# A two-layer decoder on one core: the last rows of the gated product are normalised inside the quantised stage

## The reference, cut to what matters

```
x = layernorm(x + attention(x))                  # 16 heads
x = layernorm(x + cross_attention(x, context))   # 16 heads, causal
x = layernorm(x + gated_mlp(x))                  # silu(x Wg) * (x Wu) Wd, width 1024
x = layernorm(x + quantised_attention(x))        # int4 activations in chunks of 32 rows, 32 heads
x = layernorm(x + grouped_attention(x, context))
x = layernorm(x + eight_bit_product(x))
```

## Time and profile before

| | |
|---|---|
| median of 3 runs | 2766.9 us (2765.09, 2766.90, 2777.92) |
| profiled execution | 2765.41 us, of which the span of the profile is 2763.6 us |
| busy in the span | PE 95%, DVE 69%, ACT 51%, POOL 43% |
| granted TensorE clock, mean | 0.972 |

### The profile page before, as it was taken

The page is one execution under the profiler, slowest core; times in us unless marked ns, Lnnn a source line. Parts: engine busy times, 40 slices in busy tenths (PEclk is TensorE's granted clock), DMA queues, the critical chain, the costliest instruction groups (busy, mean ns, idle before and its releaser), DMA issues. The chain is left out here.

```text
span 2763.6 us, 66143 instructions
## 1 busy us (share of the span) xinstructions
PE 2625.6 (95%) x23860; PEld 2277.5 (82%) x23860; DVE 1911.1 (69%) x4152; ACT 1413.9 (51%) x3352; POOL 1183.4 (43%) x1559
## 2 busy tenths in 40 slices
PE   7999999997899999999999969999699999999996
PEld 7999999995798888888988858888477777777775
DVE  6655565564777777777777745444599899867775
ACT  3222222223666666666666643332466666666664
POOL 2211111113667767767677630111234444444443
PEclk9999999998999999999999989999799999999997
DMA  5000000001000000000000020000100000001100
GB/s 192 9 8 8 4 8 8 8 0 62 5 6 4 4 6 4 4 6 4 6 4 4 4 80 1 0 0 0 39 9 13 8 11 11 20 29 43 38 30 24
DMA packets 43394, 49.65 MB, mean 18 GB/s; under 512 B 3952, under 2 KB 33616, under 8 KB 43056
## 3 DMA queue, kind: packets, MB, share of 16 engines
q1 hardware_dynamic: 43312, 48.55, 5.3%
HBM read 35.96 MB, written 4.19 MB: 15 GB/s over the span
## 5 line engine op out<-in xcount | busy, mean ns | idle before, releaser
L588 POOL TENSOR_TENSOR a_probs<-a_probs,a_rs 128x512 f32<-128x512 f32 x64 | 70.6, 1103 | 466.4 <-DVE a_rs L444 466.4
L1174 POOL TENSOR_TENSOR b_rows<-b_rows,b_swapped 128x512 f32<-128x512 f32 x160 | 204.7, 1288 | 56.5 <-DVE b_swapped L947 56.5
L1109 ACT ACTIVATE b_probs<-bank,b_shift,b_q_scale 128x128 f32<-128x128 f32 x512 | 228.2, 461 | 0.7
L532 ACT COPY a_pT<-bank 128x512 f32<-128x512 f32 x64 | 37.5, 586 | 308.4 <-PE bank L325 308.4
L1221 POOL TENSOR_TENSOR b_probs<-b_probs,b_rs 128x512 f32<-128x512 f32 x128 | 133.2, 1041 | 137.3 <-DVE b_rs L999 134.1
L449 DVE TENSOR_TENSOR a_oT<-bank,a_oT 128x512 fp32r<-128x512 f32 x128 | 82.5, 686 | 143.6 <-ACT a_oT L537 143.6
L955 DVE TENSOR_REDUCE b_ss<-b_squares 128x4 f32<-128x512 f32 x192 | 125.2, 680 | 73.7 <-ACT b_squares L1084 73.7
L1184 POOL TENSOR_TENSOR b_rms<-b_rms,sh_minus_half 128x8 f32<-128x8 f32 (+1 forms) x128 | 170.4, 1331 | 10.6
L46 PE MATMUL bank<-a_xT,early_wq 128*128 128x256 f32 x512 | 150.2, 293 | 13.2 <-DVE early_wq L73 10.4
L46 PE MATMUL bank<-early_wo,b_oT 128*128 128x256 f32 x512 | 150.7, 294 | 1.4 <-DVE b_oT L921 1.4
L46 PE MATMUL bank<-early_wo,a_oT 128*128 128x256 f32 x512 | 145.3, 284 | 4.0 <-DVE a_oT L449 4.0
(11 more groups left out here) (386 smaller groups left out, 9049.0 us busy)
## 6 DMA issues: line engine op xcount, KB each, us to landing
d_x_in<-sh_x SPq DMA_DIRECT2D x32, 256.0 KB, 2.4
a_xT_in<-in_xT SPq DMA_DIRECT2D x16, 256.0 KB, 2.7
sh_x<-in_x SPq DMA_DIRECT2D x1, 4096.0 KB, 18.1
b_ctx_in<-in_ctxT SPq DMA_DIRECT2D x32, 128.0 KB, 2.0
e_cT<-in_ctxT SPq DMA_DIRECT2D x32, 128.0 KB, 2.5
out<-f_res SPq DMA_DIRECT2D x16, 256.0 KB, 2.6
a_qT<-in_L_attn_Wq SPq DMA_DIRECT2D x4, 512.0 KB, 6.2
a_stage<-in_L_attn_Wo SPq DMA_DIRECT2D x1, 2048.0 KB, 13.0
```

The lines of the kernel that those rows point to most:

```text
L1109: op = act.activation(probs[:, g % 2, keys], bS[:, keys], ACT.Exp, bias=shift[:, g % 2, a:a + 1], scale=q_scale[:, g, a // 2, a % 2:a % 2 ...
L1174: pool.tensor_tensor(rows[:, unit, :], rows[:, unit, :], swapped[:, half, :], ALU.add).then_inc(added[unit], 1)
```

## The change

1. The gated block ends with the last residual sum. The moments of its last four tiles are taken by DVE as its first work of the next block (`late_stats`), and POOL normalises them during the first turn of the quantised stage, after `find_spans` of that turn (`late_normalise`). `WideRows` is made before both blocks.
2. In the first turn PE turns the two tiles from `sh.x` instead of `x_in`. The load of the first two tiles is still issued. SP waits, ahead of the load for the second turn, until the late normalisation is done.
3. The product with the value bias comes behind the first turning of rows; DVE adds it in the first turn, after `centre`. PE's three waits move from ahead of the turns to a place in the first turn, ahead of `spread_top`.
4. POOL clears `g_v` in its second turn, after `find_spans`.
5. The rows of the last sublayer's result (`f_res`) use the memory of the quantised weights' rows.

```diff
+def late_stats(dve, rows, n_tiles, done):
+
+    for r in range(n_tiles):
+        dve.bn_stats(rows.stats[:, r, :], rows.res[:, r, :]).then_inc(done, 1)
+    dve.wait_ge(done, n_tiles)
+    for r in range(n_tiles):
+        dve.bn_aggr(rows.meanvar[:, r, :], rows.stats[:, r, :]).then_inc(done, 1)
+
+
+def late_normalise(pool, rows, first_tile, n_tiles, stats_done, step, before):
+
+    n = n_tiles
+    pool.wait_ge(stats_done, 2 * n)
+    pool.tensor_scalar(rows.rstd[:, 0:n], rows.meanvar[:, 0:n, 1], LN_EPS, None, ALU.add).then_inc(step, 1)
+    pool.wait_ge(step, before + 1)
+    pool.tensor_tensor(rows.rstd[:, 0:n], rows.rstd[:, 0:n], rows.minus_half[:, 0:n], ALU.pow).then_inc(step, 1)
...
+    pool.tensor_tensor(rows.res[:, 0:n, :], rows.res[:, 0:n, :],
+                       rows.rstd[:, 0:n].unsqueeze(2).to_broadcast([128, n, D]), ALU.mult).then_inc(step, 1)
+    pool.wait_ge(step, before + 4)
+    pool.tensor_tensor(rows.x[:, first_tile:first_tile + n, :], rows.res[:, 0:n, :],
+                       rows.shift[:, 0:n].unsqueeze(2).to_broadcast([128, n, D]), ALU.subtract).then_inc(step, 1)
+    pool.wait_ge(step, before + 5)
...
@@ gated_mlp_block @@
-        wide = WideRows(sh, sb, NR)
+        wide = sh.wide
...
             turn(n_turns - 1, None, n_turns - 2)
-            row_stats(dve, wide, n_turns - 1, NR, res_ready, stats_ready, meanvar_ready)
...
-            with pool.Fori(0, n_turns) as i:
+            with pool.Fori(0, n_turns - 1) as i:
                 normalise(pool, wide, i, NR, meanvar_ready, norm_step, norm_done)
@@ tail_block @@
-        f_res = f_sb("res", [128, 2, 2, D])
+        f_res = sh.quantised.rows[:, 0:2]
...
             sh.eight.load(sp, t)
+            sp.wait_ge(zeroed, 12)
+            sp.wait_ge(x_loaded, nth(0, 1, 1, 16))
             with sp.Fori(1, n_turns) as i:
...
             pe.wait_ge(w_loaded, 16 * sh.quantised.N_LOADS)
-            for c in range(C):
-                op = pe.matmul(bP[:, 0:D], v_bias[:, c:c + 1].to_broadcast([128, 128]), w[:, O, c, :], start=(c == 0), stop=(c == C - 1))
-            op.then_inc(v_bias_through, 1)
+            def is_first(i):
+                return i is not None and type(i.n) is int and i.n == 0
+
+            def carry_v_bias():
+                for c in range(C):
+                    op = pe.matmul(bP[:, 0:D], v_bias[:, c:c + 1].to_broadcast([128, 128]), w[:, O, c, :], start=(c == 0), stop=(c == C - 1))
+                op.then_inc(v_bias_through, 1)
...
-                pe.wait_ge(x_loaded, nth(i.n, 1, 1, 16))
+                rows = sh.x if is_first(i) else x_in
+                if not is_first(i):
+                    pe.wait_ge(x_loaded, nth(i.n, 1, 1, 16))
...
-                        op = pe.transpose(bX[0][:, c * 256 + r * 128:c * 256 + (r + 1) * 128], x_in[:, r, c * 128:(c + 1) * 128], sh.ident[:, :])
+                        op = pe.transpose(bX[0][:, c * 256 + r * 128:c * 256 + (r + 1) * 128], rows[:, r, c * 128:(c + 1) * 128], sh.ident[:, :])
                 op.then_inc(qx.turned, 1)
+                if is_first(i):
+                    carry_v_bias()
...
                 turn_cmax_x(new)
+                if is_first(new):
+                    pe.wait_ge(out_bias_ready, 9)
+                    pe.wait_ge(of_chunk_ready, 1)
+                    pe.wait_ge(zeroed, 7)
                 turn_cmax_att(old)
                 spread_top(new, qx, bX[1], y_summed)
...
         def _(dve):
+            late_stats(dve, sh.wide, sh.wide.N, out_bias_ready)
             dve.wait_ge(w_loaded, 16 * sh.quantised.N_LOADS)
-            dve.wait_ge(v_bias_through, 1)
-            dve.tensor_tensor(out_bias[:, :], bP[:, 0:D], b_out[:, :], ALU.add).then_inc(out_bias_ready, 1)
+            def carry_bias():
+                dve.wait_ge(v_bias_through, 1)
+                dve.tensor_tensor(out_bias[:, :], bP[:, 0:D], b_out[:, :], ALU.add).then_inc(out_bias_ready, 1)
...
                 centre(new, qx, bX[0])
+                if new is not None and type(new.n) is int and new.n == 0:
+                    carry_bias()
...
             pool.wait_ge(zeroed, 7)
-            pool.memset(g_v[:, :, :, :, :], 0.0).then_inc(zeroed, 1)
-            pool.wait_ge(zeroed, 8)
-            for h in range(2):
-                pool.memset(g_v[h * S:(h + 1) * S, :, :, :, 2 * W + h:2 * W + h + 1], 1.0).then_inc(zeroed, 1)
             pool.wait_ge(w_loaded, 16 * sh.quantised.N_LOADS)
-            pool.wait_ge(zeroed, 10)
...
                 find_spans(new, qx)
+                if is_turn(new, 0):
+                    late_normalise(pool, sh.wide, NT - sh.wide.N, sh.wide.N, out_bias_ready, zeroed, 7)
+                if is_turn(new, 1):
+                    clear_values()
                 weigh_steps(new, qx)
```

More of the change, by code:

```diff
@@ L147, in normalise @@
     pool.sem_inc(norm_done, 1)
+def late_stats(dve, rows, n_tiles, done):
[10 more added lines that the diff above has]
+    pool.tensor_tensor(rows.rstd[:, 0:n], rows.rstd[:, 0:n], rows.minus_half[:, 0:n], ALU.pow).then_inc(step, 1)
+    pool.wait_ge(step, before + 2)
+    pool.tensor_tensor(rows.shift[:, 0:n], rows.meanvar[:, 0:n, 0], rows.rstd[:, 0:n], ALU.mult).then_inc(step, 1)
+    pool.tensor_tensor(rows.res[:, 0:n, :], rows.res[:, 0:n, :],
[4 more added lines that the diff above has]
+    pool.wait_ge(step, before + 5)
 def self_attention_block(nc, sh):
@@ L1248, with __init__, sb @@
 class WideRows:
-    def __init__(self, sh, sb, n):
+    N = 4
+    def __init__(self, sh, nc, ctx):
+        def sb(name, shape):
+            return ctx.enter_context(nc.sbuf_tensor("wide_" + name, shape, F32))
+        n = self.N
         self.x, self.minus_half, self.passed_dve, self.passed_pool = sh.x, sh.minus_half, sh.passed_dve, sh.passed_pool
@@ L1952, in _ @@
             pe.wait_ge(w_ready, 4)
-            pe.wait_ge(out_bias_ready, 1)
-            pe.wait_ge(of_chunk_ready, 1)
-            pe.wait_ge(zeroed, 7)
             def g_turn_x(i, oldest):
@@ L2244, in _ @@
             pe.wait_ge(g_w_loaded, 16 * sh.grouped.N_LOADS)
-            pe.wait_ge(zeroed, 10)
+            pe.wait_ge(zeroed, 15)
             from_first_to_second()
@@ L3009, in _, with is_turn, clear_values @@
             pool.wait_ge(zeroed, 7)
-            pool.memset(g_v[:, :, :, :, :], 0.0).then_inc(zeroed, 1)
-            pool.wait_ge(zeroed, 8)
-            for h in range(2):
-                pool.memset(g_v[h * S:(h + 1) * S, :, :, :, 2 * W + h:2 * W + h + 1], 1.0).then_inc(zeroed, 1)
             pool.wait_ge(w_loaded, 16 * sh.quantised.N_LOADS)
-            pool.wait_ge(zeroed, 10)
+            def is_turn(i, n):
+                return i is not None and type(i.n) is int and i.n == n
+            def clear_values():
+                pool.memset(g_v[:, :, :, :, :], 0.0).then_inc(zeroed, 1)
+                pool.wait_ge(zeroed, 13)
+                for h in range(2):
+                    pool.memset(g_v[h * S:(h + 1) * S, :, :, :, 2 * W + h:2 * W + h + 1], 1.0).then_inc(zeroed, 1)
+                pool.wait_ge(zeroed, 15)
             def find_bias(i, q):
@@ L3458, in program @@
             sh.quantised, sh.grouped, sh.eight = QuantisedWeights(nc, late), GroupedWeights(nc, late), EightBitWeights(nc, late)
+            sh.wide = WideRows(sh, nc, late)
             for sublayer in REST:
```

## The result

The changed kernel took 2755.7 us, median of 7 runs (2750.66 to 2761.33), against 2767.5 us for the kernel before in the same comparison (7 runs, 2764.88 to 2779.04). The ratio is 0.9945, 95% interval 0.9923 to 0.9966. A second measurement of the same kernel gave 2757.2 us (6 runs) against 2771.8 (26 runs), ratio 0.9957, 0.9941 to 0.9973. In microseconds the ratios are 15.2 (9.4 to 21.3) and 11.9 (7.5 to 16.4). They are not the quotients of the two medians, which lie 11.8 and 14.6 us apart. The forecast was 12.9 of gain and 2753.0 us.

The account below looks back on a forecast made before the run. The prediction held PE to bound the quantised stage (408 of 435 us), with a one-engine-at-a-time chain at the seam. 12.3 us there plus 0.6 for the clock made 12.9, hence 2753.0 us, range 2748 to 2760.

Parts of the forecast that it names:

- earlier start of the block: At the seam, the gated block ends with the residual sum, so the next block starts 7.46 us earlier.
- waits within the start: Between block start and POOL's bias work, shorter waits of POOL, PE and DVE give 4.9 us.
- The crossing: Between the two blocks: last operation to first of the next assumed to cost 1.07 us also when DVE is last.
- The marker: POOL's start on the bias in the first turn, L3022: forecast at 1939.2 instead of 1951.5, 12.3 us earlier.
- Taking only the load away would not have given it: At the block's start, removing the load alone would not gain the 4.9 us, since `of_chunk` ended PE's wait.
- Late normalisation hidden by 0.7 us: On POOL between `find_spans` and `weigh_steps`: 5.83 us fit into 6.53 of idleness, cost 0, bounds 0 to 1.9.
- the sign named in the prediction: On POOL in the first turn: `weigh_steps` starting straight behind the normalisation would show the prediction wrong.
- Clock, 0.6 us: PE's clock in the first turns: gain from less idleness ahead, 0.6 us taken for all.
- Rival A: First turn: DVE's `unit` or inversion waits for POOL's last normalising operation, up to 1.9 us, time 2755; 15%.
- Rival C: Block start: another engine or ACT's and SP's semaphores hold it; gain 8.0 us, time 2758; 6%.
- Rival D: Later turns: slow clock granted in most, 2.73 us each, slower from the fifth more, 2780 with ten; 2%.
- Rival B: Later turns: one or two slow-clock turns more or fewer, 2.73 us each, time 2747.5 to 2758.5; 27%, evenly.

Follow-up runs that it names:

- after: Profiled execution of the changed kernel in the first measurement, the slowest of its seven runs: 2761.33 us.
- `of_chunk` ahead: Changed kernel, but PE waits for ACT's `of_chunk` ahead of its first turn, rows still turned from `sh.x`; 2765.9 us, one run.
- the short filling: Changed kernel plus 6, 8 and 7 unread PE products behind the value bias, top's spread and first scores of the first turn; 2756.2 us, ratio 0.9943.
- again: Profiled execution of the unchanged changed kernel in its second measurement, the fastest of its runs: 2751.74 us.
- the extra power: Changed kernel plus one more power of 4 columns (1.04 us) on POOL ahead of the late normalisation; 2761.6 us, one run.
- an earlier start: Changed kernel with POOL's clearing of `v` moved into the first turn and DVE's lowest and highest ahead of the late moments; 2749.3 us, ratio 0.9938.
- the filled kernel: Changed kernel plus 26 unread PE products in the first turn, 12 behind the value bias, 14 behind `spread_top`; 2759.8 us, ratio 0.9954.
- the load put back: Changed kernel, but in the first turn PE waits for the load into `x_in` and turns the tiles from there; 2758.0 us, one run.

## Why the prediction was right, by its steps

The mechanism was the one forecast, and the parts can be set beside the terms ("after"; places are relative to the end of the residual sum):

| step of the prediction | forecast | measured |
|---|---|---|
| earlier start of the block | 7.46 us, with a crossing of 1.07 | 8.53 - 0.82 = 7.71, crossing 0.82 |
| waits within the start | 4.9 | 8.32 - 3.47 = 4.85 |
| spans to `weigh_steps`, with the late normalisation in it | 0 (6.53 hides 5.83) | 6.16 instead of 6.53, 0.37 gained; 0.08 us to spare |
| first projection to value projection | part of the clock's 0.6 | 5.18 to 4.75, 0.43 gained |
| sum | 12.9 | 13.4; 12.9 of it to the first projection, where 12.3 were forecast |

The level, 2753.0 us, was missed by 2.7 and 4.2 us (2755.7 and 2757.2). Part of that is the starting point: the forecast took 2766.9 us of three runs for the kernel before, and the later medians were 2767.5 and 2771.8. Whether the gain is within 0.5%, to which the prediction gave 0.60, is not settled: the two ratios stand at 0.55% and 0.43%.

- *The crossing.* The one assumption made for want of a row. It was 0.81 to 0.82 us in every kernel whose block ended with DVE's sum, and 1.07 again in the one that ended with POOL.
- *The marker.* 1938.43, forecast 1939.2. Of the difference 0.53 us are that execution's earlier residual sum and 0.25 the crossing.
- *Taking only the load away would not have given it.* Right: with `of_chunk` ahead the marker did not move at all, and not to wait for `x_loaded` is worth 2.2 us once that wait is gone.
- *Late normalisation hidden by 0.7 us.* Right in its result, with less room than stated. The prediction had the thresholds 5.9 us behind the spans, after the last normalising operation. In "after" they came 5.49 behind them, 0.07 us before the subtraction's end at 5.56, and lost nothing by it only because they are 0.22 us long; 0.08 us of delay was left. In the kernels where the clock stood at 1.00 in that stretch (the short filling, `of_chunk` ahead) the thresholds were held 1.2 us. There the sign named in the prediction, `weigh_steps` straight behind the normalisation, did occur; in "after" and "again" it didn't. So the 0 holds for the clock that PE had there: 0.72 from the spans to the thresholds in "after", 1.00 in the other two. The bound of 0.7 us for a full clock was of the right kind and measured 6.53 - 6.09 = 0.44.
- *Clock, 0.6 us.* Measured 0.80 in "after" and 0.20 in "again", so the value lies between two executions and no more can be said for it. In "after" the spreading product took 0.80 us at clock 1.00 instead of 1.42 at 0.50, more than the whole 0.37; in "again" it took 1.42, and the 0.27 gained there came from the turning of the spans before it, 0.64 instead of 1.07. The projections stayed at the low level for their first part in both, as forecast, and their stretch gained 0.43 in "after" and nothing in "again" (5.25 against 5.18). This term was sized for the seam alone.
- *Moved product, `out_bias`, clearing, SP's wait.* Nothing, as forecast. In "after" `g_v` is cleared at 1965.10 in 7.5 us of POOL's free time (5.88 were left behind it), the product runs at 1935.61, `of_chunk` is rounded at 1939.65 + 0.83, ahead of its use.
- *Rival A* is refuted by "after" itself and by the extra power: the case occurred in both and cost nothing. *Rival C* did not occur in the changed kernel; only with "an earlier start" did a semaphore that SP raises hold DVE. *Rival D* did not either: what looked like it in "after" was absent in "again". *Rival B* is what one sees from execution to execution: 10.8 us in fifteen turns of "after", which is four turns of 2.73 and not the one or two that I had allowed for. The sign given for it (more than two turns above 27 us) occurred in "after", 10 against 6, and not in "again", 6. Taken as falling on both kernels alike it widens each median and doesn't shift their ratio. That is argued from two executions of one kernel and one of the other, and not shown: the fifteen turns of only one execution of the kernel before are on record.

On rival A: the rows and the Trainium skill agree about the two-input operations. The Trainium skill, SBUF — State Buffer, section "Who interferes with whom", has them exclude a GpSimd instruction that reads this memory, and the thresholds (1.09 us instead of 0.22) and `exceed` (1.85 instead of 0.27) show it. For `unit` I had taken from that section that `tensor_scalar` may take part. The row says 0.15 us within the product. The Trainium skill, VectorE: DVE Perf Modes, section "Mode 2×_2P", gives the condition that I had left out: the access pattern is split in half along its outermost dimension that isn't one. That a single column has nothing to split is my reading; the Trainium skill has no example of it. Read so, it speaks against rival A from the start, and the trace agrees (0.15 us inside the product).

What stays open: what makes the clock fall in one turn and not in the same turn of the next execution. Filling the seam did not settle it: with it the second turn ran at 0.79 and 0.82.

## What to carry to other kernels

Where a stage's last engines work alone before all engines meet, move that work to the far side and into the first idle stretch of its own engine, and compute the slack first, up to the instruction that the moved work can hold on another engine and not only up to the next one in its own queue: here 5.8 us fitted into 6.5 with 0.6 left by the second count and 0.08 by the first. When several waits are in line, price each by taking only it away: turning the rows without their load was worth nothing before the wait for `of_chunk` had moved. Compare two profiles by distances between instructions from a common point, not by their spans, as soon as a repeated run of one kernel scatters by as much as the change is worth.

## What the runs showed of the hardware

- A higher mean clock is no sign of faster work when idle time was removed. The stretch from residual sum to first projection had a granted clock of 0.54 over 27.79 us before and of 0.79 over 14.85 us after. Taking it out raises the mean over the span by (27.79 x 0.46 - 14.85 x 0.21) / 2760 = 0.0035, and the runs' medians are 0.9695 (26 runs) and 0.974 (13). So most of the 0.0045 between them is the absent idle time. The rows, before and after:
```profile
1934.67:1962.46 27.79, 7.33 (x38) 4.55 (x39) 8.12 (x25) 1.82 (x4) 12.22 (x23) 0.54 0.23 75
```
```profile
1934.14:1948.99 14.85, 5.08 (x38) 3.14 (x38) 8.05 (x25) 1.82 (x4) 10.80 (x20) 0.79 0.44 140
```
- The granted clock also stood at its low level while PE was busy without a gap: 3.00 of 3.00 us in the filled kernel, where it had been 1.00 until 1946 and PE had last stood idle for 1.35 us up to 1944.36; and in the kernel before in this window of a later turn, with PE's last idle time 0.30 us, up to 2263.35:
```profile
2264.00:2271.00 7.00, 7.00 (x38) 4.97 (x37) 5.48 (x10) 3.38 (x6) 2.85 (x9) 0.53 0.09 33
```
- A DVE operation with two inputs in the on-chip memory that started inside a wide two-input operation of POOL lasted until that one's end (0.22 became 1.09 and 1.42 us, 0.27 became 1.85); a one-column `tensor_scalar` or inversion there took its 0.15.
- SP raised 66 semaphores one by one in 4.3 us (1936.4 to 1940.7 in the kernel with the load put back). What waits for one of them early in a block waits for its place in that row: DVE until 1.4 us into the block ("an earlier start"), PE, by its row, until 3.0.
- A crossing between two blocks took 0.81 to 0.82 us when DVE was last (eleven traces), 1.07 when POOL was (two).
